# Gated cross-attention kernel: in the first attention, the sums' matmuls are issued ahead of the products with the values

## The reference, cut to what matters

```python
q = _fq_sym(q, axis=-1); k = _fq_sym(k, axis=-1); v = _fq_sym(v, axis=2)
attn = jnp.einsum('bhqd,bhkd->bhqk', q, k)
attn = jax.nn.softmax(attn.astype(jnp.float32), axis=-1)
attn = _fq_unsigned(attn, axis=-1)      # rounded to 255 levels of the row's maximum
out = jnp.einsum('bhqk,bhkd->bhqd', attn, v)
```

## Time and profile before

| | |
|---|---|
| median of three runs | 6699.94 us (6691.82 to 6702.1) |
| profiled execution, its own time | 6694.85 us |
| span of its trace | 6692.8 us |
| PE matmul busy | 5788.9 us (86%) |
| DVE busy | 5604.2 us (84%) |
| ACT busy | 4493.5 us (67%) |
| POOL busy | 3706.5 us (55%) |
| mean granted clock of PE | 0.919 |

### The profile page before, as it was taken

One profiled execution on the slowest core, in us unless ns is written; L12 is line 12 of the kernel. 1 busy time (PEld: TensorE's weight loads), 2 busy tenths in 40 slices (PEclk: granted clock), 3 DMA queues, 4 the chain that ended last, 5 costly groups with the idle time before them and its releaser, 6 DMA issues. The chain is left out here.

```text
span 6692.8 us, 179938 instructions
## 1 busy us (share of the span) xinstructions
PE 5788.9 (86%) x64153; PEld 2456.4 (37%) x64160; DVE 5604.2 (84%) x8840; ACT 4493.5 (67%) x4358; POOL 3706.5 (55%) x3978
## 2 busy tenths in 40 slices
PE   2874999999999999999999999999969486999723
PEld 2651233333333333333333333333344353544411
DVE  4877999999999899899999989999963556777765
ACT  0660588988898899898889988988932012666401
POOL 2331488888788788788888878878820001000000
PEclk7995799999999999999999999999979697999866
DMA  1544101101101001011011011010010078877600
GB/s 58 124 121 125 18 9 23 21 8 26 18 11 25 15 16 25 10 21 22 10 24 20 9 27 18 11 25 14 15 36 0 17 291 197 117 110 113 97 29 10
DMA packets 176564, 315.49 MB, mean 47 GB/s; under 512 B 91731, under 2 KB 137812, under 8 KB 171042
## 3 DMA queue, kind: packets, MB, share of 16 engines
q1 hardware_dynamic: 175656, 303.45, 21.2%
HBM read 192.39 MB, written 113.07 MB: 46 GB/s over the span
## 5 line engine op out<-in xcount | busy, mean ns | idle before, releaser
L1163 DVE TENSOR_REDUCE a_mx<-PS 128x1 f32<-128x512 f32 x6620 | 4072.9, 685 | 235.9 <-PE PS L1047 232.3
L1134 ACT ACTIVATE a_e<-PS,a_sk 126x1024 f32<-126x1024 f32 x3264 | 3634.0, 1114 | 490.2 <-PE PS L1030 141.6
L901 POOL TENSOR_SCALAR a_p<-a_e 126x1024 f16<-126x1024 f32 x3264 | 3412.9, 1046 | 677.8 <-ACT a_e L1134 624.7
L1030 PE MATMUL PS<-a_Q,a_K 54*126 54x512 bf16 x6528 | 2109.9, 404 | 32.2 <-issue 23.0
L1047 PE MATMUL PS<-a_K,a_Q 48*128 48x512 bf16 (+1 forms) x6884 | 2106.7, 383 | 30.9 <-POOL a_p L866 30.6
L1074 PE MATMUL PS<-a_e,a_sel 126*32 126x256 f32 x26112 | 1994.1, 382 | 27.2 <-issue 27.2
L1030 PEld LDWEIGHTS PS<-a_Q,a_K 54*126 54x126 bf16 x6528 | 614.6, 131 | 1382.9 <-issue 1323.9
L1070 PE MATMUL PS<-a_p,a_V 128*32 128x256 f16 x13056 | 960.0, 284 | 14.6 <-ACT a_og L1115 10.5
L1070 PEld LDWEIGHTS PS<-a_p,a_V 128*32 128x32 f16 x13056 | 336.8, 93 | 1250.4 <-POOL a_p L901 1053.3
L1074 PEld LDWEIGHTS PS<-a_e,a_sel 126*32 126x32 f32 x26112 | 756.0, 110 | 37.1 <-issue 30.7
L2120 DVE TENSOR_REDUCE b_mx<-PS 128x1 f32<-128x512 f32 x803 | 504.4, 684 | 188.7 <-PE PS L2004 188.7
(11 more groups left out here) (330 smaller groups left out, 3435.9 us busy)
## 6 DMA issues: line engine op xcount, KB each, us to landing
b_K<-d_k SPq DMA_DIRECT2D x210, 200.1 KB, 6.2
a_K<-d_k SPq DMA_DIRECT2D x99, 400.2 KB
d_v<-v1v SPq DMA_DIRECT2D x9, 3328.0 KB, 10.3
b_V<-d_v SPq DMA_DIRECT2D x36, 832.0 KB, 12.4
d_k<-k_T SPq DMA_DIRECT2D x100, 252.0 KB, 4.1
d_k<-k1p SPq DMA_DIRECT2D x54, 400.2 KB, 7.0
a_V<-d_v SPq DMA_DIRECT2D x68, 204.0 KB, 2.8
d_v<-vq SPq DMA_DIRECT2D x17, 803.2 KB
```

Source lines behind the costliest of these rows:

```text
L901: g.tensor_scalar(p[0:rows, kk % RE, :], e[0:rows, kk % RE, :], 1.0, SHIFT, ALU.mult, ALU.add).then_inc(rounded, 1)
L1030: last = pe.matmul(self.PS[0:key_rows(s), e_bank(i, s) + y, :], Kb[0:E_ROWS, (i // NC) % 2, s * KT:s * KT + key_rows(s)], Qb[0:E_ROWS, i % ...
L1134: a.activation(e[0:r, kk % RE, :], self.PS[0:r, e_bank(i, s):e_bank(i, s) + 2, :], ACT.Exp, scale=skb[0:r, hb, s:s + 1]).then_inc(exp_done, 1)
L1163: v.tensor_reduce(mx[:, col:col + 1], bank, AX.X, ALU.max).then_inc(max_done, 1)
```

## The change

Within `av` the four sums are issued first. They wait for `exp_done` of this tile (and for tile 0 for `gathered`) and clear the bank at tile 0. The waits for `rounded` and `ld_v` follow, then the four products, whose last one closes the accumulation at the last tile and increments `av_done`. Nothing is added or removed but one more wait in each `av` (on `exp_done`), and `order` stays as it is.

```diff
                 def av(g, i, t, first_ever):
 
                     n, kk = g * IB + i, i * NE + t
+                    pe.wait_ge(exp_done, g * (IB * NE) + kk + 1)
+                    if t == 0 and not first_ever:
+                        pe.wait_ge(gathered, n)
+                    for j in range(4):
+                        pe.matmul(self.PS[32 * j:32 * j + 32, O_BANK, 0:QW], sel[0:key_rows(t), :],
+                                  e[0:key_rows(t), kk % RE, j * QW:(j + 1) * QW], start=(t == 0),
+                                  stop=False, tile_position=(0, 32 * j), skip_group_check=True)
                     pe.wait_ge(rounded, g * (IB * NE) + kk + 1)
-                    if t == 0:
-                        if not first_ever:
-                            pe.wait_ge(gathered, n)
-                        if i % NC == 0:
-                            pe.wait_ge(ld_v[i // NC], 16 * V_DMAS * (g + 1))
+                    if t == 0 and i % NC == 0:
+                        pe.wait_ge(ld_v[i // NC], 16 * V_DMAS * (g + 1))
                     for j in range(4):
-                        pe.matmul(self.PS[32 * j:32 * j + 32, O_BANK, 0:QW], Vb[:, i // NC, t, :],
-                                  p[:, kk % RE, j * QW:(j + 1) * QW], start=(t == 0), stop=False,
-                                  tile_position=(0, 32 * j), skip_group_check=True)
-                    for j in range(4):
-                        last = pe.matmul(self.PS[32 * j:32 * j + 32, O_BANK, 0:QW], sel[0:key_rows(t), :],
-                                         e[0:key_rows(t), kk % RE, j * QW:(j + 1) * QW], start=False,
-                                         stop=(t == NE - 1), tile_position=(0, 32 * j), skip_group_check=True)
+                        last = pe.matmul(self.PS[32 * j:32 * j + 32, O_BANK, 0:QW], Vb[:, i // NC, t, :],
+                                         p[:, kk % RE, j * QW:(j + 1) * QW], start=False, stop=(t == NE - 1),
+                                         tile_position=(0, 32 * j), skip_group_check=True)
                     last.then_inc(av_done, 1)
```

## The result

The changed kernel takes 6751.52 us (median of 4 runs, 6748.28 to 6759.15), before 6701.02 (4 runs): a ratio of 1.0082, 95% interval 1.0069 to 1.0095, so 50 us slower. In a second series of five runs it was 6749.23 against 6695.22, again 1.0082 (1.0068 to 1.0095). The forecast was 6767, the range 6729 to 6805.

The account below looks back on a forecast made before the run. PE's serial order was taken as the bound, at 1.228 us a step; 3200 stretches of av at +0.021 us gave +67 us on 6694.85, and 5 more for the runs' median: 6767 us, range 6729 to 6805.

Parts of the forecast that it names:

- rival C: Products' weight load: the wait for POOL is real, sums fill it, 365 us less, 6335 us; chance 0.02.
- The price per step: PE's order inside av: from its start to e0 0.678 us instead of 0.657, so +0.021 us a step.
- e1 to sums: Switch from e1, PE's matmul with 126-column weights just before av, to av's start: distance stays at 0.306 us.
- the first pass: Sums' first float32 pass, now first behind the shape switch after e1: about 403 ns in place of 382.
- last sum to last product: Inside av, within the 32-column shape: last product starts 0.214 us after the last sum, without a gap.
- last product to e0: Switch from av to e0, PE's next matmul: e0 starts 0.203 us after the last product, at most 0.213.
- Rival A: Switch behind e1: the drain hides the sums' float32 load, -0.012 us a step, 38 us less, 6662 us; chance 0.04.
- B: Switch behind e1: sums pay 10 ns as products do, -0.002 us a step, -6 us, 6694 us; chance 0.08.
- D: Products' load shows behind the sums: +0.103 us a step on top, 330 us more, 7097 us; chance 0.02.
- The other engines: Beside PE: DVE and ACT idle more, by about 0.02 us a step.
- The count: 100 stretches of av between switches per chunk, 32 chunks: 3200 stretches, times 0.021 us gives 67 us.
- gathered* ahead of the sums ... 0: Tile 0 of a chunk: PE idles for ACT's copy as before, then the same two av follow; cost 0.

Follow-up runs that it names:

- The extra wait: Kernel before the change, products first, with only the added wait on exp_done between products and sums: 6697.8 us against 6695.16, ratio 1.0002.
- the 16-bit pair: Two kernels with sums of rounded 16-bit values and 16-bit weights, computing other denominators: products first 6509.75 us, sums first 6512.28; against before 0.9721 and 0.9727.
- the alternation: Against the kernel before: sums first in odd key tiles only, products first in even ones: 6719.34 us, ratio 1.0038.
- e0's wider load: Scores' weights loaded 128 columns wide instead of 126: order of before 6585.61 us, 0.9838 against before; changed order 6653.62 us, 0.9937.

## Why the prediction was right

- **The bound.** PE's serial order set the step before and after; in steps 8 to 97 PE's loads wait for DVE not once in either profile (the 129.7 us of such waits before, and 130.6 after, lie at the chunks' ends and starts). Right.
- **The label "waits for POOL"** as no wait, from the count of roundings. Right: nothing of 1053 us was gained, and the label moved on to ACT (rival C out).
- **The price per step.** 0.021 forecast, 0.0234 measured. Its parts: e1 to sums 0.306, measured 0.306; the first pass 403, measured 403; last sum to last product 0.214, measured 0.216; last product to e0 0.203, for which there was no row, measured 0.204. The last sum stands 0.260 behind the first, where 0.261 was put. Rival A (the drain covers the load) and B (both loads cost alike) fall with the 403; D with the last product 0.216 behind the last sum, where it asked for 0.317.
- **What made it so.** That the rise came from the float32 load, and not from the order or the wait, was an inference from L2039. The extra wait and the 16-bit pair show that it is neither the wait nor the order, the alternation that it is paid step by step. That within the float32 matmul it is the load is supported by e0's wider load and by the sizes, and not isolated.
- **The other engines.** ACT idles more by 60 us, 0.019 a step, as forecast. DVE was to idle more too and does not; its records overlap less. That sign was wrong, and nothing in the sum hung on it.
- **The count.** 3200 stretches, confirmed by steps 8 to 97 (2880 of them lose 67.5).
- **The total.** +67 forecast, +50 to +54 measured. The miss is in "*gathered* ahead of the sums ... 0" and in the line that took the price at the half clock to be all that the clock could do: I kept the number of half-clock stretches fixed. With fewer of them, and a shorter stall at the loop's edge, 14 to 25 us came back in the two profiles; the step itself was sized 8 us too low over the kernel, which hid a part of that. That the total landed so near is in that part luck.

## What to carry to other kernels

Where a program changes the shape in which it uses the array, look at what stands first behind the change: it pays for the end of its weight load. In these traces it lasts longer than the same matmul elsewhere by 10 or 11 ns with a load of 93, by 24 with one of 106 to 109, and by 50 with one of 128. So some 80 ns of the load cost nothing (an estimate from these differences), and what is longer is paid. Put the shortest load there (16 bit, or a full 128 columns) and let the long one hide behind other work in the same shape. And before a wait in a list is believed, count: number the producer's and the consumer's instructions up to one moment, and see which one was really needed.

## What was not expected of the hardware

The clock at one and the same idle place of the program fell in 5 to 6 chunks in each of three profiles with the products first, and in 0 to 2 in each of three with the sums first, after about the same 0.4 us of idle time. It is not a rule of the order: with 16-bit sums it was 7 and 5, with `av` in pairs 3 and 7. What decides it is open.
